# Linear attention on Gram matrices: the product of the means cut into sixteen 32-square blocks, its tokens' part by batch groups, and x loaded with its column of ones

## The reference

```python
for i in range(12):
    q, k, v = split(x @ Wqkv[i].T + bqkv[i])          # heads of 8 channels
    att = einsum('bhqd,bhkd->bhqk', q, k) / sqrt(8)
    y = einsum('bhqk,bhkd->bhqd', att, v)
    x = y @ Wproj[i].T + bproj[i] + x
x = layernorm(x0 + x)
x = layernorm(x + (silu(x @ wg.T) * (x @ wu.T)) @ wd.T)
```

## Time and profile before

| | |
|---|---|
| median of three runs | 336.1 us |
| the profiled execution | 335.32 us |
| its span from the first to the last instruction | 333.5 us |
| time of that execution around the span | 1.8 us |
| mean granted TensorE clock | 0.999 |
| PE busy | 317.8 us (95%), 3336 passes |
| weight loads busy | 288.9 us (87%) |
| DVE busy | 226.4 us (68%) |
| ACT busy | 183.0 us (55%) |
| POOL busy | 96.6 us (29%) |
| DMA | 13.66 MB, mean 41 GB/s |

### The profile page before, as it was taken

The page is one execution under the profiler, slowest core; times in us unless marked ns, Lnnn a source line. Parts: engine busy times, 40 slices in busy tenths (PEclk is TensorE's granted clock), DMA queues, the critical chain, the costliest instruction groups (busy, mean ns, idle before and its releaser), DMA issues.

```text
span 333.5 us, 8348 instructions
## 1 busy us (share of the span) xinstructions
PE 317.8 (95%) x3336; PEld 288.9 (87%) x3336; DVE 226.4 (68%) x638; ACT 183.0 (55%) x417; POOL 96.6 (29%) x89
## 2 busy tenths in 40 slices
PE   8899999999999999999999999999999999999993
PEld 7879889798897998979979799797997988888873
DVE  1167676775775757757677576676765569998974
ACT  3338757376483774846738467385572164444550
POOL 2006046050320502305023050140505034555533
PEclk9999999999999999999999999999999999999999
DMA  8751001010010200102002010020000000111112
GB/s 232 267 220 61 4 2 61 2 63 2 2 61 3 63 0 3 63 0 63 2 2 62 2 52 12 2 62 2 2 3 2 0 1 0 31 48 46 33 34 67
DMA packets 10660, 13.66 MB, mean 41 GB/s; under 512 B 512, under 2 KB 8832, under 8 KB 10496
## 3 DMA queue, kind: packets, MB, share of 16 engines
q1 hardware_dynamic: 8368, 11.94, 11.4%
q10 hardware_dynamic: 2256, 1.21, 1.3%
HBM read 11.04 MB, written 2.10 MB: 39 GB/s over the span
## 4 chain that ended last, share of the span: by engine, by line
PE 80%; DVE 9%; issue 3%; DMA 3%; ACT 2%; POOL 1%; ACTq 0%; POOLq 0%; DVEq 0%
PE ps L797 14%; PE ps L850 13%; PE ps L885 13%; PE ps L748 6%; PE ps L746 6%; PE ps L747 6%; PE ps L964 3%; PE ps L806 3%; PE ps L836 3%; DMA xt<-x_tok 3%; DVE s_rows L581 3%; PE ps L813 2%; DVE xt L681 2%; DVE mt L574 2%; PE ps L953 1%
## 5 line engine op out<-in xcount | busy, mean ns | idle before, releaser
L346 POOL TENSOR_TENSOR step_lo<-step,step_hi 128x512 fp32r<-128x512 f32 x44 | 54.9, 1279 | 180.3 <-ACT step_hi L430 180.3
L746 PE MATMUL ps<-state_hi,step_hi 128*128 128x258 f32 x176 | 50.7, 288 | 0.0
L850 PE MATMUL ps<-s_rows,w 32*128 32x256 f32 x768 | 44.8, 380 | 5.5 <-DVE s_rows L581 5.5
L748 PE MATMUL ps<-state_hi,step_lo 128*128 128x258 f32 x176 | 49.9, 283 | 0.0
L747 PE MATMUL ps<-state_lo,step_hi 128*128 128x258 f32 x176 | 49.6, 282 | 0.0
L850 PEld LDWEIGHTS ps<-s_rows,w 32*128 32x128 f32 x768 | 40.4, 185 | 7.4 <-ACT s_rows L424 7.4
L430 ACT CAST step_hi<-step 128x512 fp32r<-128x512 f32 x44 | 27.0, 619 | 33.8 <-DVE step L586 33.8
L797 PE MATMUL ps<-w,gram 128*128 128x128 f32 x352 | 44.0, 278 | 0.0
L797 PEld LDWEIGHTS ps<-w,gram 128*128 128x128 f32 x352 | 41.1, 192 | 1.0
L885 PE MATMUL ps<-step,gram 128*128 128x128 f32 x320 | 40.6, 281 | 0.0
L885 PEld LDWEIGHTS ps<-step,gram 128*128 128x128 f32 x320 | 37.3, 192 | 3.3 <-DVE step L586 3.3
(11 more groups left out here) (103 smaller groups left out, 502.7 us busy)
## 6 DMA issues: line engine op xcount, KB each, us to landing
w<-weights SPq DMA_DIRECT2D x12, 496.5 KB, 3.5
xchan<-x_chan SPq DMA_DIRECT2D x1, 2048.0 KB, 10.6
out<-xchan SPq DMA_DIRECT2D x7, 256.0 KB, 2.4
xt<-x_tok ACTq DMA_DIRECT2D x4, 256.0 KB, 7.5
xt<-x_tok SPq DMA_DIRECT2D x4, 256.0 KB, 5.3
fw_int<-ffn_weights SPq DMA_DIRECT2D x1, 576.0 KB, 4.8
out<-xchan SPq DMA_DIRECT2D x2, 128.0 KB, 2.4
cst<-consts ACTq DMA_DIRECT2D x1, 154.5 KB, 4.4
```

The source lines that it names most:

```text
L346: nc.gpsimd.tensor_tensor(group(step_lo, g), group(step, g), group(step_hi_f, g), ALU.subtract).then_inc(step_lo_ready, 1)
L746: nc.tensor.matmul(dst, l_hi, r_hi, start=True, stop=False)
L748: return nc.tensor.matmul(dst, l_lo, r_hi, start=False, stop=True)
L850: last = nc.tensor.matmul(n_banks(h)[:, k, :], w[r, s, WQ + P * i:WQ + P * (i + 1)], s_rows[r, h, i, :], start=i == 0, stop=i == QUADS - 1)
```

## The change

- **Means.** `means` becomes 128 columns: for each group of four batches a block of 32, of which 8 are filled (four means with bias, four without) and the rest are zero. `rows_stage` is one product of 128x128 by 256 columns, so that `rows` holds the group's means in 32 rows of its own. `vdiag` is gone, `kdiag` is one instruction of 512 columns with the signs in its factor, and `m_means` is sixteen products of 32 rows by 32 columns of the array, 128 moving columns each: group i's rows into bank `M_BANKS[i]`, quarter q of the partitions.
- **M by groups.** M has one bank a group (6, 7, 4, 5), `m_tokens` and `take_blocks` run once per group, on 128 columns. The products of gram and k of the last two groups move to banks 0 and 1, `rows` to bank 6. `s_stage(0)` waits for M of groups 0 and 1 in turn, `s_stage(1)` for all four.
- **The order of batches** in PSUM is plain now: an `add_identity` reads a part of all four banks of its half, so that the products behind wait for both of a half (`2 * (g // 2) + 2`).
- **x** lies in HBM with its ones, 516 floats in a row for four tiles, and is loaded so; the constants' DMA moves to SP behind the first weights. The weights' rows grow from 993 to 1185 floats, since the biases of k and v are no longer cut in four.

The core of the diff:

```diff
-        GK_BANKS = (2, 3, 6, 7)
-        ROWS_BANK = 0
-        M_BANKS = (1, 5)
+        GK_BANKS = (2, 3, 0, 1)
+        ROWS_BANK = 6
+        M_BANKS = (6, 7, 4, 5)
...
-                sp.dma_start(xt[:, per * i:per * (i + 1), 0:P], x_v[:, per * i:per * (i + 1), :]).then_inc(x_in[i], 16)
+                sp.dma_start(xt[:, per * i:per * (i + 1), :], x_v[:, per * i:per * (i + 1), :]).then_inc(x_in[i], 16)
             sp.dma_start(w[:, 0, :], weights[0]).then_inc(w_in[0], 16)
+            sp.dma_start(cst[:, :], consts).then_inc(cst_in, 16)
...
-                nc.vector.tensor_tensor(rows[:, :], ps[:, ROWS_BANK, 0:2 * QUAD], w[:, s, BK:BK + 2 * QUAD],
+                nc.vector.tensor_tensor(rows[:, :], ps[:, ROWS_BANK, 0:2 * P], w[:, s, BK:BK + 2 * P],
                                         ALU.add).then_inc(rows_ready, 1)
                 dve.wait_ge(rows_ready, at(1, 1))
-                nc.vector.tensor_tensor(vdiag[:, :, :], rows[:, QUAD:].unsqueeze(1).to_broadcast([P, QUADS, QUAD]),
-                                        own_quad.unsqueeze(2).to_broadcast([P, QUADS, QUAD]), ALU.mult)
...
+                nc.vector.tensor_tensor(kdiag[:, :, :], rows[:, 0:P].unsqueeze(1).to_broadcast([P, GB, P]),
+                                        one_hot.unsqueeze(2).to_broadcast([P, GB, P]), ALU.mult).then_inc(kdiag_ready, 1)
...
+                def take_blocks(g):
+                    dve.wait_ge(m_done, at(GROUPS, g + 1))
+                    nc.vector.tensor_tensor(group(mt, g), ps[:, M_BANKS[g], 0:P].rearrange("p (b i) -> p b i", b=GB),
+                                            blk.unsqueeze(1).to_broadcast([P, GB, QUAD]), ALU.mult).then_inc(m_ready, 1)
...
-                def m_means(h):
-                    nc.tensor.matmul(ps[:, M_BANKS[h], 0:n * QUAD], vdiag[:, :, :].rearrange("p q c -> p (q c)"),
-                                     kdiag[:, n * h:n * (h + 1), :], start=True, stop=False)
+                def m_means():
+                    for i in range(GROUPS):
+                        for q in range(QUADS):
+                            own, r = slice(QUAD * i, QUAD * (i + 1)), slice(QUAD * q, QUAD * (q + 1))
+                            nc.tensor.matmul(ps[r, M_BANKS[i], 0:P], rows[own, P + QUAD * q:P + QUAD * (q + 1)],
+                                             kdiag[own, :, r], start=True, stop=False)
+                def m_tokens(g):
+                    pe.wait_ge(gk_ready, at(GROUPS, g + 1))
+                    for q in range(QUADS):
+                        r = slice(QUAD * q, QUAD * (q + 1))
+                        last = nc.tensor.matmul(ps[r, M_BANKS[g], 0:P], w[:, s, WV + QUAD * q:WV + QUAD * (q + 1)],
+                                                gk[:, GB * g:GB * (g + 1), r], start=False, stop=True)
+                    last.then_inc(m_done, 1)
...
-                    pe.wait_ge(step_ready, at(GROUPS, g + 1))
+                    pe.wait_ge(step_ready, at(GROUPS, 2 * (g // 2) + 2))
```

More of the change, by code:

```diff
@@ L57 @@
 BQ = (QUADS + 3) * P
[L58 removed]
+BK, BV, BP = BQ + QUAD, BQ + QUAD + P, BQ + QUAD + 2 * P
 WCOLS = BP + 1
[L61 to L62 removed]
+C_ID, C_PROJ, C_BLK, C_HOT = 0, P, 2 * P, 2 * P + QUAD
+C_ONE = C_HOT + GB
 CCOLS = C_ONE + 1
@@ L122, in build @@
         mbq = sb("mbq", [P, BATCHES])
-        rows = sb("rows", [P, 2 * QUAD])
-        kdiag = sb("kdiag", [P, BATCHES, QUAD])
-        vdiag = sb("vdiag", [P, QUADS, QUAD])
+        rows = sb("rows", [P, 2 * P])
+        kdiag = sb("kdiag", [P, GB, P])
         shift = sb("shift", [P, BATCHES, 2])
-        means = sb("means", [P, 2, BATCHES])
-        mu = means[:, 0, :]
-        means_by_batch = means[:, :, :].rearrange("p k b -> p b k")
+        means = sb("means", [P, GROUPS * QUAD])
+        means_by_group = means[:, :].rearrange("p (g r) -> p g r", r=QUAD)[:, :, 0:2 * GB].rearrange("p g (k b) -> p g k b", k=2)
         mu0 = sb("mu0", [P, BATCHES])
@@ L273, in one_product, with mu_column, by_group @@
             return ps[:, k, P * (b % GB):P * (b % GB + 1)]
+        def mu_column(b):
+            return means[:, QUAD * (b // GB) + b % GB:QUAD * (b // GB) + b % GB + 1]
+        def by_group(part):
+            return part.rearrange("p (g b) k -> p g k b", b=GB)
         def s_banks(h):
@@ L585, in add_identity @@
                         dve.wait_ge(n_done, at(2, g // 2 + 1))
-                    nc.vector.tensor_tensor(group(step, g).rearrange("p (k j) c -> p k j c", j=2),
-                                            n_banks(g // 2)[:, 2 * (g % 2):2 * (g % 2) + 2, :].rearrange("p k (j c) -> p k j c", j=2),
-                                            (project if last else ident).unsqueeze(1).unsqueeze(1).to_broadcast([P, 2, 2, P]),
+                    j = g % 2
+                    nc.vector.tensor_tensor(group(step, g), n_banks(g // 2)[:, :, P * j:P * (j + 1)],
+                                            (project if last else ident).unsqueeze(1).to_broadcast([P, GB, P]),
                                             ALU.add).then_inc(step_ready, 1)
-                take_blocks(0)
-                take_blocks(1)
+                for g in range(GROUPS):
+                    take_blocks(g)
                 take_s(0)
                 take_s(1)
-                dve.wait_ge(m_ready, at(2, 2))
+                dve.wait_ge(m_ready, at(GROUPS, GROUPS))
                 nc.vector.tensor_tensor(bqp[:, :, :], mt[:, :, :],
@@ L819, in rows_stage @@
                     pe.wait_ge(mu_ready, at(PAIRS, PAIRS))
-                    for q in range(QUADS):
-                        r = slice(QUAD * q, QUAD * (q + 1))
-                        last = nc.tensor.matmul(
-                            ps[r, ROWS_BANK, 0:2 * QUAD], means[:, :, :].rearrange("p k b -> p (k b)"),
-                            w[:, s, WK:WK + 2 * P].rearrange("p (k c) -> p k c", k=2)[:, :, r], start=True, stop=True)
-                    last.then_inc(mean_done, 1)
+                    nc.tensor.matmul(ps[:, ROWS_BANK, 0:2 * P], means[:, :], w[:, s, WK:WK + 2 * P], start=True, stop=True)\
+                        .then_inc(mean_done, 1)
                 def s_stage(h):
-                    pe.wait_ge(m_ready, at(2, h + 1))
                     for j in range(2):
+                        pe.wait_ge(m_ready, at(GROUPS, GROUPS if h else j + 1))
                         for i in range(QUADS):
                             r = slice(QUAD * i, QUAD * (i + 1))
-                            place = n * h + QUADS * j
+                            place = GB * (2 * h + j)
                             last = nc.tensor.matmul(s_banks(h)[:, i, P * j:P * (j + 1)],
@@ L861, in layer @@
                 pe.wait_ge(b_lo_ready, at(PAIRS, PAIRS))
-                pe.wait_ge(kdiag_ready, at(2, 2))
-                m_means(0)
-                m_means(1)
-                pe.wait_ge(gk_ready, at(GROUPS, 2))
-                m_tokens(0)
-                pe.wait_ge(gk_ready, at(GROUPS, GROUPS))
-                m_tokens(1)
+                pe.wait_ge(kdiag_ready, at(1, 1))
+                m_means()
+                for g in range(GROUPS):
+                    m_tokens(g)
                 if last_layer:
@@ L1034, in lay_out @@
     wts[:, :, BK:BP] = 0
-    for q in range(QUADS):
-        quad, rows = slice(QUAD * q, QUAD * (q + 1)), slice(QUAD * q, QUAD * q + BATCHES)
-        wts[:, rows, BK:BK + QUAD] = bqkv[:, None, P:2 * P][:, :, quad]
-        wts[:, rows, BV:BV + QUAD] = bqkv[:, None, 2 * P:3 * P][:, :, quad]
+    for g in range(GROUPS):
+        wts[:, QUAD * g:QUAD * g + GB, BK:BP] = bqkv[:, None, P:]
     wts[:, :, BP] = bproj
```

72 lines of the change are left out of this document (25 added, 47 removed).

## The result

The changed kernel takes 327.12 us, median of four runs (326.16 to 327.99), against 336.18 (335.86 to 336.31) for the kernel before in the same comparison: a ratio of 0.9731, 95% interval 0.9699 to 0.9763. In a later comparison the same kernel took 327.56 (326.99 to 330.38) against 336.38, ratio 0.9767 (0.9715 to 0.9818).

What follows compares the result with a forecast made beforehand. TensorE's passes were taken as the bound (PE 80% of the chain), other engines counting only where it leaves PE. Layers 5.0 and start 1.9 took 335.32 to 328.4, or 329.2 against the median; range 327.6 to 336.4.

Steps and rivals of the forecast that it cites:

- The likeliest case: M's means: all 16 array places work by themselves, first to last start 0.32 us; the forecast, 54%.
- T: M's means: time from the first to the last start of the 32 block passes, taken as 0.32 us.
- T of 0.65, 0.90 and 1.8: M's means: row quarters in turn (0.65 us, 16%), four at a time (0.90, 9%), blocks in program order (1.8, 11%).
- the slower side: Whole kernel: the chance that the change makes it slower, 0.14.
- the slower rival: M's means: blocks start in program order, each waiting for the former's second pass; 346.9 us in all, 11%.
- a gain of 0.42 forecast: Each layer: 0.34 us from M's means plus 0.08 from the tokens; twelve layers give 5.0 us.
- first step 0.21: Start of a PE stage: first step takes 0.21 us because its weights were not loaded ahead; read from s_stage.
- The drain: PE between passes of different cut: each change of cut costs about 0.1 to 0.2 us.
- the s_rows wait: Layer, s_stage over DVE's copy of s_rows to n_stage: stays as before, PE's wait unchanged at about 0.46 us.
- the waits for step: Products gram times step: waiting for two adds costs nothing while n_stage covers it, uncovered up to 0.6 us a layer.
- the tokens' wait for gk: Token products: gk of group 3 is there at 188.04, its passes due at 187.87 + 0.77; no wait.
- The start: Start of the kernel: PE no longer waits twice for x, gaining 1.9 us, bounds 1.5 and 2.1.

Runs made afterwards that it cites:

- tokens of 64: The changed kernel with a group's token products as two of 64 output columns instead of four of 32, result not the reference's: one run, 327.27 us.
- the start alone: The kernel before with only the new start (x with its ones in 2064 B rows, constants behind the first weights on SP): 333.93 us, ratio 0.9932.
- after: The changed kernel with the whole change, against the kernel before: 327.12 us, ratio 0.9731; its profiled execution took 327.99 us.
- the second profile of after: The changed kernel itself run and profiled once more, nothing changed, in a later comparison with the kernel before: 327.56 us, ratio 0.9767.
- the constants alone: The kernel before with only the constants' DMA moved to SP's queue behind the first weights, x still in 512 B rows: one run, 334.21 us.

## Why the prediction was too cautious

**The mechanism was right.** The likeliest case was that the sixteen places work by themselves, and it came so: the 32 starts, both passes of all places, lie within 0.50 - 0.27 = 0.23 us (the row of L799 in PE's timeline, less its last pass), in either order of rows and columns. The rivals' T of 0.65, 0.90 and 1.8 are excluded by that row alone, and with 1.8 the slower side. The program-order rule of the Trainium skill ("TensorE: Matmul & The Clock Gate", Part 3) does not hold pass by pass, as the slower rival took it: blocks of one row quarter start 7 ns apart, and sixteen passes of 0.292 us have started before the first of the sixteen of 0.267, so that second passes do not hold up the blocks behind them. Block by block the trace doesn't contradict the rule. Nor do weight loads wait for another row quarter: those of the first four blocks, all of one, start at 180.949 to 180.968, 7 ns apart, beside the first block's pass. The 4 ns a tile of the same page of the Trainium skill is not met either; with 16 places the stagger is 7 ns, as it was with four.

**The step that failed is the layer's: a gain of 0.42 forecast, 0.61 measured.** The mechanism held, and one term of the sum was mis-sized: the "first step 0.21" of a stage, which I read from s_stage and used for every stage whose weights are not ahead. It measured 0.134. It counts twice:

- In T. Sixteen first passes start within 15 x 0.007 = 0.10, as forecast. The second sixteen start 0.134 behind the first, not 0.21. T is 0.233, not 0.32: 0.09.
- In the tokens. Their second set starts at 0.134, too. DVE has its first piece 181.88 - 181.38 = 0.50 after the tokens' start, forecast 0.58; s_stage starts at 1.03, forecast 1.11: 0.08.

What the step is made of shows in the widths: rows before (64 columns streamed, 32 of weights) 0.080, tokens and blocks (128, 32) 0.134, tokens of 64 (128, 64) 0.160, s_stage (128, 128) 0.214, tokens before (256, 32) 0.240. All five are the weights' columns / 1.2 GHz plus one pass's streaming (0.053, 0.107 and 0.213 for 64, 128 and 256 columns). That is a rule fitted to four of them and met by the fifth, the 0.160, which was forecast before its run; why it is so, no run shows. The rows to see it were there: the earlier trace rows has four and eight token passes of before, 0.42 and 0.64. I took from them the interval of a set and not the step (0.64 less a last pass of about 0.38 and 0.02 is 0.24). The remaining 0.02 of the 0.19 is the rows stage and rounding. Twelve times 0.19 is 2.3 us, and 329.2 - 2.3 = 326.9 lies below the range: this term alone is enough for the miss.

One reading beside it was wrong and cost nothing: DVE's four pieces of M were taken one behind the other, 4 x 0.29 = 1.17, and took 0.94, since they start 0.22 apart. DVE then waits for s_stage in any case.

**The drain was right.** Each change of cut costs what I took: blocks 0.21 behind the last k pass (180.95 - 180.74), tokens 0.20 behind the last block pass (181.38 - 181.18). As forecast, too, were the s_rows wait (0.84), the waits for step (none) and the tokens' wait for gk (none).

**The start was right in what it removed, and off by what it uncovered.** Forecast 1.9 with bounds 1.5 to 2.1; 1.6 in the first profile, 1.0 in the second, 2.0 with the order of blocks changed and in the start alone. x came faster than the 294 GB/s that I had reckoned with at worst: 399 to 406 GB/s from 3 to 9 us with packets of 2064 B. It landed a little later than I had worked out, and still ahead of PE: the fourth pair at 5.9 to 6.2 (forecast 5.6), the last at 9.5 to 9.8 (9.1). The first pair came at 4.4 to 4.7 instead of 4.2, which takes 0.2 to 0.4 from the gain. The rest is the pace of the first gram passes, below. My reason, the packets' size and the constants, stands in both parts: the order of the queue took the waits away, and the packets' size keeps the last pair out of PE's way once PE runs at full pace.

**The sum.** With the sizes measured: 335.32 - 7.3 - 1.6 - 0.2 = 326.2 for an execution like the profiled one of before, and 336.2 - 9.1 = 327.1 against the median, measured 327.1. That it fits so closely is luck: the start differs by 1.0 between profiles, the end by 1.3, and stalls come and go. The range's low end took the forecast's terms as nearly exact while its high end reached for every rival. The first step was a term I had not bounded, since it seemed read and not assumed.

## What to carry to other kernels

- Many small products on different places of the array cost their starts: here 7 ns for each of the first sixteen blocks and 17 ns for each beyond. Then cut the work so that a stage's passes are few per place, and count the step to the second set separately.
- A duration read in one stage holds for another only if what it consists of has the same size. Before carrying a number over, look for a stage whose row differs from it in one size; here the tokens' rows stood beside s_stage's and give 0.240 where that has 0.214, so that the step is no constant.
- In a start whose loads race against PE, first ask what stands ahead in the queue of the load that is waited for. Then ask whether the other engine ran at full pace when the wait was gone: here a slow start of PE hid what the packets' size is worth. And give an estimate an error on both sides even where every rival lies on one.

## What the runs showed of the hardware

**TensorE starts at half its pace.** In each profile but the start alone the first gram passes start 0.214 us apart, and the later ones 0.112: nearly a ratio of two, as the levels of 1.2 and 2.4 GHz have. The views print a granted clock of 1.00 for all of this, but ahead of the clock's first record in a trace that is no measurement. The first record is at 5.76 us in after, 4.95 with the blocks' order changed, 6.76 in the second profile of after, 6.57 with the constants alone and 4.35 in the start alone, and it is there that the pace changes. In all of them PE had been busy with its passes on the zero tile, 0.214 apart as well, from 1.06 to 4.42. PE from the first gram pass, of after and of the kernel with the blocks' order changed, up to 5.6 us:

```profile
4.46 1.43 PE L756 MATMUL ps<-xt 128*128 128x129 f32 x5
```

```profile
4.44 1.39 PE L756 MATMUL ps<-xt 128*128 128x129 f32 x8
```

Five slow passes in the first, one in the second, nine in the second profile of after, none in the start alone. Each costs 0.1, and the first k pass follows it: 12.32, 11.92, 12.94, and 11.97 with a first gram pass at 4.72. In the kernel before PE's waits for x hid this; now it is most of the spread of the start between these profiles.

**PE stalls for 0.3 to 2.6 us near fetches of instructions.** After has 3792 passes and 30 fetches of 16 KB where before has 3336 and 27. The stalls named "issue" in PE's rows came in the first layer (1.08, 2.56), in the middle (0.72) and in the last layer (0.26, and 0.3 that follow from it), each during a fetch or within 1.2 us behind the end of one. None over 0.2 us is in the three profiles with the old layers. Most fetches pass without a stall, and no run moves or removes one, so that the fetch is the cause is argued, not shown. More passes mean more fetches, and this may be why after's runs spread over 1.8 to 3.4 us and those of before over 0.5 to 1.8. That is argued as well.

**A stall can cost more than its length.** Behind the one of 2.56 us the granted clock fell to 0.50 for 3.4 us, and that cost another 1.4.
